# Attention with joined products for v's two parts, and one of eight pairs of heads weighed in float32

## What is computed

```python
q, k, v = (qkv[:, :, 0], qkv[:, :, 1], qkv[:, :, 2])          # 16 heads of 32
attn = jnp.einsum('bnhd,bmhd->bhnm', q, k) * SCALE
attn = jnp.where(causal, attn, NEG)
attn = jax.nn.softmax(attn, axis=-1)
out = jnp.einsum('bhnm,bmhd->bnhd', attn, v).reshape(B, N, C)
return _bitlinear(out, w_proj)      # rounds out to 8 bits by its row's maximum, w_proj to three values
```

## Time and profile before

| | us |
|---|---|
| median of 3 runs | 1661.09 (1660.46 to 1661.43) |
| the profiled execution | 1663.5 |
| its span on the core | 1661.7 |
| attention, first to last start of `row_max` | 67 to 508 |
| first matmul of the mixing stage | 556.9 |

### The profile page before, as it was taken

How to read it: one execution, slowest core, us unless ns; L and a number is a source line. 1 busy time by engine, 2 the same in 40 slices (tenths; PEclk the granted TensorE clock), 3 DMA queues, 4 the chain that set the end, 5 groups by cost and what they waited for, 6 DMA issues and landing times.

```text
span 1661.7 us, 27064 instructions
## 1 busy us (share of the span) xinstructions
PE 1519.7 (91%) x10503; PEld 876.0 (53%) x10581; DVE 1298.7 (78%) x1865; ACT 665.6 (40%) x1190; POOL 972.9 (59%) x706
## 2 busy tenths in 40 slices
PE   2698898989988678799999999999999999999998
PEld 2477777777776233344444444444444444444443
DVE  5698898899885579888778878887878878878621
ACT  4577777777767110322322222223222222232131
POOL 2378778887775356655645644654564465465242
PEclk9799999999999889999999999999999999999999
DMA  3544543645431611200120030020020020010000
GB/s 130 150 126 124 137 131 101 155 120 130 124 87 53 177 45 51 69 20 7 27 68 7 13 83 7 14 76 13 14 64 25 7 70 26 1 45 1 0 26 26
DMA packets 62048, 105.98 MB, mean 64 GB/s; under 512 B 7880, under 2 KB 14176, under 8 KB 61920
## 3 DMA queue, kind: packets, MB, share of 16 engines
q1 hardware_dynamic: 61728, 104.10, 23.3%
q10 hardware_dynamic: 192, 0.14, 0.1%
HBM read 50.74 MB, written 19.92 MB: 43 GB/s over the span
## 4 chain that ended last, share of the span: by engine, by line
PE 59%; DVE 4%; POOL 2%; issue 1%; ACT 0%; POOLq 0%; DVEq 0%
PE gu L665 20%; PE y L630 10%; PE gu L679 9%; PE y L633 3%; PE y L638 3%; PE gu L618 3%; PE y L637 3%; PE y L634 3%; PE y L636 3%; PE misc L645 1%; PE misc L655 1%; PE misc L594 1%; PE misc L538 1%; DVE z L975 1%; DVE oT L986 1%
## 5 line engine op out<-in xcount | busy, mean ns | idle before, releaser
L1440 POOL TENSOR_TENSOR pL<-pT,pH 128x768 f16<-128x768 f32 x128 | 220.1, 1721 | 90.1 <-PE pv L513 40.3
L1532 POOL TENSOR_TENSOR fuL<-fu,fuH 128x512 f16<-128x512 f32 x96 | 125.1, 1304 | 248.1 <-ACT fuH L1345 248.1
L630 PE MATMUL y<-kv,toep 128*128 128x512 f32 x496 | 242.6, 612 | 20.1 <-DVE z L975 17.9
L986 DVE TENSOR_REDUCE oT<-z 128x64 f32<-128x512 f32 x256 | 175.6, 686 | 8.8
L665 PE MATMUL gu<-fT,wg 128*128 128x512 f16 x768 | 181.4, 379 | 0.4 <-ACT fT L1364 0.4
L665 PE MATMUL gu<-fT,wu 128*128 128x512 f16 x768 | 181.4, 379 | 0.0
L982 DVE TENSOR_TENSOR z<-z,cT 128x512 f32<-128x512 f32 x112 | 168.2, 1502 | 3.8
L1345 ACT ACTIVATE fuH<-fu 128x512 f16<-128x512 f32 x96 | 60.2, 627 | 254.7 <-DVE fu L1001 254.7
L1191 ACT ACTIVATE pT<-s_kq,ws 128x768 f32<-128x768 f32 x128 | 115.3, 901 | 104.8 <-PE s_kq L493 104.8
L979 DVE TENSOR_TENSOR z<-y,shared 128x512 f32<-128x512 f32 x112 | 76.8, 686 | 90.8 <-PE y L634 76.9
L630 PEld LDWEIGHTS y<-kv,toep 128*128 128x128 f32 x496 | 92.7, 195 | 101.5 <-issue 62.0
(11 more groups left out here) (189 smaller groups left out, 3777.8 us busy)
## 6 DMA issues: line engine op xcount, KB each, us to landing
pack<-qkhl SPq DMA_DIRECT2D x256, 128.0 KB, 2.6
x_sb<-in_x SPq DMA_DIRECT2D x16, 512.0 KB, 4.7
c_sb<-in_ctx SPq DMA_DIRECT2D x32, 256.0 KB, 4.8
hankel<-in_L_xattn_k SPq DMA_DIRECT2D x32, 256.0 KB, 4.8
x_grp<-x_scratch SPq DMA_DIRECT2D x32, 256.0 KB, 4.0
out_y<-yo SPq DMA_DIRECT2D x32, 256.0 KB, 2.9
x_scratch<-x_sb SPq DMA_DIRECT2D x15, 512.0 KB, 3.0
wraw<-in_L_attn_w_qkv SPq DMA_DIRECT2D x3, 1024.0 KB, 9.9
```

Source lines behind the costliest of these rows:

```text
L630: made = T.matmul(to, tap(h, lb - kb), keys_values(h, kb, half), start=kb == 0, stop=kb == lb)
L986: V.tensor_reduce(out=oT[h % 2][:, lb, own].rearrange("p (b j) -> p b j", b=HB), in_=z[n % 2][:], op=ALU.add, axis=AXIS.X).then_inc(m_z, 1)
L1440: G.tensor_tensor(pL[n % 2][:], pT[n % NP][:], pH[n % NP][:], ALU.subtract).then_inc(low_done, 1)
L1532: G.tensor_tensor(fuL[:, ib, :], fu[n % 2][:], fuH[:, ib, :], ALU.subtract).then_inc(f_fl, 1)
```

## The change

It joins v's high and low part in one tile `vHL` of 65 columns (32 high, a one, 32 low), so that a block of probabilities takes two matmuls of 65 columns (`pH` and `pL` times both parts) where it took four. The two halves of the sum land apart in PSUM and in `oraw`, ACT copies 260 columns where it copied 132, and a new POOL instruction, `sum_parts`, adds them, once a batch, at step 8b+21. DVE's division moves from step 8b+21 to 8b+22, and waits for that sum (`o_sum`).

The pair p = 0 of each batch is weighed without a split: six float32 matmuls of 33 columns, straight from `pT` and a float32 v (`vW`). It has no high and no low part. The high part of p = 4 moves from DVE to ACT, so DVE has none left. `split_v` on DVE has three instructions where it had two (448, 64 and 448 columns where it had twice 512). `pT` has four buffers where it had three; the buffers of `fw_raw` go from three to two, so that SP's load of piece n waits for POOL to be through with piece n-2.

```diff
-    NX, NPACK, NP = 8, 3, 3
-    HIGH_ON_ACT = (1, 2, 3, 5, 6, 7)
+    NX, NPACK, NP, NPT = 8, 3, 3, 4
+    W_HEADS = 2
...
-        oraw = [q(f"oraw{i}", [P, NT, HEADS, VW], F32) for i in range(2)]
-        fw_raw = [q(f"fw_raw{i}", [P, PIECE], F32) for i in range(3)]
+        oraw = [q(f"oraw{i}", [P, NT, HEADS, VW + D], F32) for i in range(2)]
+        fw_raw = [q(f"fw_raw{i}", [P, PIECE], F32) for i in range(2)]
...
-        vH = [q(f"vH{i}", [P, NT, HEADS, VW], F16) for i in range(3)]
-        vL = [q(f"vL{i}", [P, NT, HEADS, D], F16) for i in range(3)]
+        vHL = [q(f"vHL{i}", [P, NT, HEADS - W_HEADS, VW + D], F16) for i in range(3)]
+        vW = [q(f"vW{i}", [P, NT, W_HEADS, VW], F32) for i in range(3)]
...
-        pT = [q(f"pT{i}", [P, 6, P], F32) for i in range(3)]
+        pT = [q(f"pT{i}", [P, 6, P], F32) for i in range(NPT)]
...
+        def whole(n):
+            return n % PAIRS == 0
...
             def weigh(n):
...
+                if whole(n):
+                    w.wait_ge(exp_done, n + 1)
+                    w.wait_ge(v_whole, 2 * b + 2)
+                else:
+                    w.wait_ge(high_done, n_split(n))
+                    w.wait_ge(low_done, n_split(n))
...
-                            T.matmul(acc[:, t, hh, :], ph[:, block, :], vh[:, mt, h, :], start=mt == 0, stop=False)
-                            T.matmul(acc[:, t, hh, 0:D], ph[:, block, :], vl[:, mt, h, :], start=False, stop=False)
-                            T.matmul(acc[:, t, hh, 0:D], pl[:, block, :], vl[:, mt, h, :], start=False, stop=False)
-                            made = T.matmul(acc[:, t, hh, :], pl[:, block, :], vh[:, mt, h, :], start=False, stop=mt == t)
+                            if whole(n):
+                                made = T.matmul(acc[:, t, hh, 0:VW], pT[n % NPT][:, block, :], vW[b % 3][:, mt, h, :],
+                                                start=mt == 0, stop=mt == t)
+                                continue
+                            v = vHL[b % 3][:, mt, h - W_HEADS, :]
+                            T.matmul(acc[:, t, hh, :], ph[:, block, :], v, start=mt == 0, stop=False)
+                            made = T.matmul(acc[:, t, hh, :], pl[:, block, :], v, start=False, stop=mt == t)
...
             def split_v(b, t):
...
+                V.tensor_scalar(vhl[:, :, 0:D], v[:, W_HEADS:, :], scale, None, ALU.mult).then_inc(v_high, 1)
+                V.tensor_scalar(vw[:, :, 0:D], v[:, 0:W_HEADS, :], scale, None, ALU.mult).then_inc(v_whole, 1)
...
-            def high_part(n):
-                w.wait_ge(exp_done, n + 1)
-                if n >= NP:
-                    w.wait_ge(pv_pe, n - NP + 1)
-                V.tensor_copy(pH[n % NP][:], pT[n % NP][:]).then_inc(high_dve, 1)
...
                 if k == 0:
                     w.wait_ge(pv_out, PAIRS * (b + 1))
                     chain.step(V.reciprocal(rl, oraw[b % 2][:, :, :, D]))
+                elif k == 1:
                     chain.wait()
+                    w.wait_ge(o_sum, b + 1)
...
             def exponentials(n):
...
-                if n >= NP:
-                    w.wait_ge(low_done, n - NP + 1)
+                if n >= NPT and whole(n - NPT):
+                    w.wait_ge(pv_pe, n - NPT + 1)
+                elif n >= NPT:
+                    w.wait_ge(low_done, n_split(n - NPT))
...
             def weighed(n):
...
+                width = VW if whole(n) else VW + D
+                h = heads_of(n)[0]
+                S.activation(oraw[b % 2][:, :, h:h + 2, 0:width], acc[:, :, :, 0:width], ACT.Copy).then_inc(pv_out, 1)
...
-                if (n := pair(t, HIGH)) is not None and n % PAIRS in HIGH_ON_ACT:
+                if (n := pair(t, HIGH)) is not None and not whole(n):
                     high_part(n)
...
+            def sum_parts(b):
+                raw = oraw[b % 2][:, :, W_HEADS:, :]
+                w.wait_ge(pv_out, PAIRS * (b + 1))
+                G.tensor_tensor(raw[:, :, :, 0:D], raw[:, :, :, 0:D], raw[:, :, :, VW:VW + D], ALU.add).then_inc(o_sum, 1)
...
             for t in STEPS:
-                if (n := pair(t, LOW)) is not None:
+                if (n := pair(t, LOW)) is not None and not whole(n):
                     low_part(n)
+                for b, k in batches(t, FINISH, 1):
+                    sum_parts(b)
...
                 wT_ready(w, 3)
-                if n >= 3:
-                    w.wait_ge(fw_taken, n - 2)
+                if n >= 2:
+                    w.wait_ge(fw_taken, n - 1)
```

More of the change, by code:

```diff
@@ L113, in decoder_kernel @@
         skips = sb(ctx, "skips", [P, M_HEADS, M_POS], F32)
-        rows_s = sb(ctx, "rows_s", [2 * IB, P], F32)
         GROUP = 4
@@ L247, in decoder_kernel @@
         st_pe, exp_done = signal("st_pe"), signal("exp")
-        high_act, high_dve, low_done = signal("p_high_act"), signal("p_high_dve"), signal("p_low")
+        high_done, low_done = signal("p_high"), signal("p_low")
+        v_whole, o_sum = signal("v_whole"), signal("o_sum")
         pv_pe, pv_out = signal("pv_pe"), signal("pv_out")
@@ L315, in decoder_kernel, with heads_of, n_split @@
         W_REST = range(min(len(weight_steps), W_STEPS), W_STEPS)
-        def high_done(n):
-            b, p = divmod(n, PAIRS)
-            if p in HIGH_ON_ACT:
-                return high_act, b * len(HIGH_ON_ACT) + HIGH_ON_ACT.index(p) + 1
-            other = [i for i in range(PAIRS) if i not in HIGH_ON_ACT]
-            return high_dve, b * len(other) + other.index(p) + 1
+        def whole(n):
+            return n % PAIRS == 0
+        def heads_of(n):
+            return 2 * (n % PAIRS), 2 * (n % PAIRS) + 1
+        def n_split(n):
+            return n - n // PAIRS
         def wT_ready(w, i):
@@ L484, in probabilities @@
                 w.wait_ge(mT_low, use + 1)
-                for hh in range(2):
-                    h = 2 * p + hh
+                for hh, h in enumerate(heads_of(n)):
                     for tile in range(2):
                         scores(s_kq[:, 2 * hh + tile, :], h, tile, tile, False)
-                    T.matmul(s_kq[:, 2 * hh:2 * hh + 2, :], pick[:, h % H_HEADS, :], nt[:, 0:N], start=False, stop=hh == 1)
-                for hh in range(2):
-                    h = 2 * p + hh
+                    T.matmul(s_kq[:, 2 * hh:2 * hh + 2, :], pick[:, 2 * (p % HP) + hh, :], nt[:, 0:N], start=False, stop=hh == 1)
+                for hh, h in enumerate(heads_of(n)):
                     scores(s_kq[:, 4 + hh, :], h, 0, 1, hh == 0)
-                    made = T.matmul(s_kq[:, 4 + hh, :], pick[:, h % H_HEADS, :], nt[:, P:N], start=False, stop=hh == 1)
+                    made = T.matmul(s_kq[:, 4 + hh, :], pick[:, 2 * (p % HP) + hh, :], nt[:, P:N], start=False, stop=hh == 1)
                 made.then_inc(st_pe, 1)
@@ L849, in weight_pieces @@
                 if not second and n < PIECES:
-                    raw, pw = fw_raw[n % 3], fw_pow[n % 2]
+                    raw, pw = fw_raw[n % 2], fw_pow[n % 2]
                     wT_ready(w, 3)
-                    w.wait_ge(fw_in[n % 3], 16 * (n // 3 + 1))
+                    w.wait_ge(fw_in[n % 2], 16 * (n // 2 + 1))
                     if n >= 2:
@@ L900, in vector_program @@
                         low_max(use)
-                if (n := pair(t, HIGH)) is not None and n % PAIRS not in HIGH_ON_ACT:
-                    high_part(n)
                 for b, k in batches(t, FINISH, 13):
@@ L1196, in high_part @@
                     w.wait_ge(pv_pe, n - NP + 1)
-                S.activation(pH[n % NP][:], pT[n % NP][:], ACT.Copy).then_inc(high_act, 1)
+                S.activation(pH[n % NP][:], pT[n % NPT][:], ACT.Copy).then_inc(high_done, 1)
             def weighed(n):
                 b, p = divmod(n, PAIRS)
-                acc = pv[:, 0:NT * 2 * VW].rearrange("p (t h w) -> p t h w", t=NT, h=2)
+                acc = pv[:, 0:NT * 2 * (VW + D)].rearrange("p (t h w) -> p t h w", t=NT, h=2)
                 w.wait_ge(pv_pe, n + 1)
@@ L1204, in weighed @@
                     w.wait_ge(o_mult, b - 1)
-                S.activation(oraw[b % 2][:, :, 2 * p:2 * p + 2, :], acc, ACT.Copy).then_inc(pv_out, 1)
+                width = VW if whole(n) else VW + D
+                h = heads_of(n)[0]
+                S.activation(oraw[b % 2][:, :, h:h + 2, 0:width], acc[:, :, :, 0:width], ACT.Copy).then_inc(pv_out, 1)
             def finish(b, k):
@@ L1624, in load_piece @@
                 wT_ready(w, 3)
[L1625 to L1627 removed]
+                if n >= 2:
+                    w.wait_ge(fw_taken, n - 1)
+                Y.dma_start(fw_raw[n % 2][:], (w_gate, w_up)[m][cb * P:(cb + 1) * P, o * PIECE:(o + 1) * PIECE]).then_inc(fw_in[n % 2], 16)
             def weight_pieces(k):
```

48 lines of the change are left out of this document (23 added, 25 removed).

## The result

The changed kernel takes 1664.7 us in the median of 14 runs (1660.8 to 1667.9), the kernel before 1661.1 (1659.6 to 1663.1): a ratio of 1.0019, interval 1.0011 to 1.0028. It is 3.7 us slower, where 10 us less were forecast. With 14 runs each, executions of one kernel spread by 0.2 to 0.4%, more than the 0.1% that three runs had suggested. The profiled span is 1663.2 against 1661.7, so the two traces show 1.5 of the 3.7.

A forecast was written before the change was run, and what follows sets the result against it. Attention was taken as bound by PE in about 76% of steps, by DVE in 24%. Savings of 0.86 us a batch, 13.8 over 16, less 1.2 (end) and 2.6 (clock), gave 10 off 1661: 1651 us, range 1640 to 1667.

The forecast's parts named there:

- the bunching of division and maximum: DVE, kind 6: both instructions (1.23 + 1.22 us), 0.95 for take_max and the scaling were said to fit in one step.
- The wait for DVE's maximum: PE's wait in attention for DVE's maximum, 31.1 us before, was to stay near 31 us or fall slightly.
- the third rival: Both savings, PE's and DVE's, count in full: 16 x 1.1 = 18 us less, 1641 us; chance 0.13.
- PE: Weighing: joined pairs 0.35 us each (0.25 saved), float32 pair 1.36 (0.77 more); 1.0 us less a batch.
- the upper bound of 0.192: Float32 pair on PE: if its weight loads don't overlap, 12 x 0.192 = 2.3 us, 1.7 more a batch.
- 0.76 less 0.3 for ACT: Per batch in attention: PE's 1.0 us counted in 76% of steps, minus 0.3 for waits on ACT's chain to xqT.
- DVE: 0.4 a batch: Of DVE's net saving of 1.25 us a batch, a third falls where DVE sets the step: 0.4.
- ACT: ACT gets 1.7 us more a batch; 0.3 charged, as PE's waits for xqT in kind 0 grow.
- The first rival: ACT becomes the bound, its 1.7 us a batch standing on the path: 1674 us, slower; chance 0.18.
- The new wait: DVE's division waits for sum_parts (1.9 us) on POOL; covered by 0.7 us, nothing counted except for the last batch.
- The end: Last batch's division, on the chain to the mixing stage, starts 1.2 us later; attention's last row_max near 496 instead of 508.
- The clock: PE's growing idle time lowers its granted clock in two such stretches more, at 1.3 us: 2.6 us lost.

The follow-up runs named there:

- no_sum_kind5: Changed kernel without sum_parts and its wait (products with v's low part missing from output), division back in kind 5 (step 8b+21): 1643.7 us, ratio 0.9896.
- no_sum_kind6: Changed kernel without sum_parts and its wait (products with v's low part missing from output), division left in kind 6 (step 8b+22): 1662.1 us, ratio 1.0003.

## Why the prediction was wrong

**The step that failed** is the sentence on DVE that priced the bunching of division and maximum at nothing: "which fits, since DVE is through early with kind 5". The numbers were against it: 0.95 + 1.23 + 1.22 and 0.68 for the scaling make 4.1 us, and PE needs 3.7 in a step of kind 6 and 2.9 in one of kind 7 (runs without pieces). By itself that excess of 0.4 costs nothing in the steady stretch; with a piece in the step or the one before it has no room left, and a DVE instruction that starts while POOL's is running waits it out (last section). That DVE is idle in kind 5 is of no use to kind 6, because `take_max` can't start before its scores are there, and the queue is in order. The move cost 18.4 us where the sum is left out; with the sum, 14.5 together with the sum's place. The wait for DVE's maximum, said to stay near 31 us, went to 35.6, and to 38.4 with that for `qkt`.

**The rest of the sum** stood nearer, and added up to about the third rival. Without the bunching and the sum the changed kernel is at 1643.7, 17.4 us under before (rival 3: 1641); I had 13.8 for it.

- PE: 0.36 a joined pair (forecast 0.35) and 1.26 for the float32 pair (1.36): right. By the rule on weight loads from the Trainium skill, "TensorE: Matmul & The Clock Gate", section "LDWEIGHTS (loading the stationary operand)", columns / 1.2 ns, the records would be 0.107 apart; the trace agrees, with 0.105. As to the bounds, the upper bound of 0.192 was wrong. What reached the steps is 0.35 a batch without pieces, against 0.76 less 0.3 for ACT, 0.46. Into kinds 7, 0 and 1 nothing was saved.
- DVE: 0.4 a batch was too small. With pieces `no_sum_kind5` gains 14.3 us in the steady stretch (350.2 to 335.9), 1.2 a batch, of which PE has 0.35. The rest, over 0.8, is twice what I gave DVE. Part of it is the clock, whose cost between 100 and 488 us falls from 8.3 to 3.4 us; which part isn't separated.
- ACT: the wait for `xqT` stayed at 2.5 us with pieces and went from 3.6 to 5.8 without. Together with those for `oraw` and `pT` it grew by 5.8 us without pieces, 0.4 a batch: right in size. The first rival, ACT as the bound, had the right sign and the wrong engine.
- The new wait: in the steady stretch nothing waited for `o_sum`, as forecast. Behind it the last three divisions waited 0.14, 4.65 and 1.51 us, where I had allowed for the last alone. The sum took 1.79 us (forecast 1.9). I had counted nothing for it in the steps; its 2.6 us are hardly clear of noise, and the traces of the changed kernel and `no_sum_kind6` have 1.8 of them in the steady stretch.
- The end, against the earlier trace rows:

```profile
535.32 0.35 DVE L831 RECIPROCAL osmall<-oraw 128x32 f32<-128x32 f32 x1 [5.82 <-ACT oraw L1215]
535.36 1.73 POOL L1455 TENSOR_TENSOR oraw<-oraw 128x896 f32<-128x896 f32 x1 [1.47 <-ACT oraw L1215]
537.18 1.23 DVE L837 TENSOR_TENSOR o_sb<-oraw,osmall 128x1024 f32<-128x1024 f32 x1 [1.51 <-POOL oraw L1455]
...
543.74 3.42 PE L541 MATMUL misc<-wprojT,oqT 128*128 128x512 bf16 x8 [0.83 <-ACT oqT L1240]
```

The division starts 1.86 us after the reciprocal where it was 0.70: 1.2 later, as forecast. What was missed is the clock behind it: the projection takes 3.42 us at a granted clock of 0.55 where it took 1.89 at 1.00. Attention was 1.4 us ahead at the last `row_max` (506.96 against 508.38, not 496), and the mixing stage starts at 558.33, 1.4 late. So the bunching ate up the gain, and the loss that the two traces show lies wholly behind the last `row_max`: 51.4 us from there to the mixing stage where it was 48.5.

- The clock: two stretches more were allowed for, 2.6 us. Between 100 and 488 us it took up to 8.3 before and 10.0 after, and the projection's 1.5 come to it: about right.

## What to carry to other kernels

Where engines run in lockstep, one step at a time, a move is priced by the fullest step it makes, not by the engine's mean load or by idle time in the step before: add up every instruction of that queue between two of the instructions the other engine waits for, the optional ones too, and compare with the other engine's step. A long optional piece of work in such a queue should be cut up and spread before anything is shaved off the main work; here that gave 16 to 23 us, more than the change could. And when several small results may be summed later, start the sum early for all but the last, so that what depends on it needn't move.

## What the runs showed of the hardware

DVE waits for POOL's running instruction, inside its own duration. The second instruction of a weight piece, first in the kernel before with POOL idle, then in the changed kernel beside the sum:

```profile
332.25 0.43 DVE L857 TENSOR_SCALAR fw_pow<-fw_pow 128x512 f32<-128x512 f32 x1
...
329.86 1.93 POOL L1455 TENSOR_TENSOR oraw<-oraw 128x896 f32<-128x896 f32 x1
330.23 1.85 DVE L865 TENSOR_SCALAR fw_pow<-fw_pow 128x512 f32<-128x512 f32 x1
```

The same instruction takes 0.43 or 1.85 us, and in the second case ends 0.3 after POOL's. That is no accident: of its 24 instances in the changed kernel 17 take 1.37 to 1.85 us, and all of these end 0.28 to 0.29 after a POOL instruction that was running when they started; the other seven take 0.43, with no POOL instruction of more than two columns beside them. The longest five divisions (1.73 to 2.60 us) end 1.08 to 1.09 after such a one. It holds the other way too: a `low_part` begun 0.19 us into the division at 130.64 takes 2.62 us in place of 1.64, and ends 1.50 after it. So these instructions are not slowed evenly: their time is what it is alone, plus the wait for the other's end. Taking the sum away (`no_sum_kind6`) brings the group's mean from 1474 to 1223 ns, but that of L863 goes from 937 to 1043 and that of the division from 1363 to 1491: what meets what is shuffled, and the three together fall by only 1.4 us in the stretch from 110 to 484. A mean duration of such an instruction is therefore a mean over two cases, and what it costs depends on which POOL instruction is running when it starts. The division had 1.23, 1.75 and 2.60 us in the lines above. The maximum of `o_sb`, with one input, stays at 1.21 to 1.22 in all of them. The Trainium skill, "GPSIMD Engine Reference", section "1. Specifications", says that the SBUF interfaces are shared and that DVE instructions with two SBUF inputs, or in a mode that uses two ports, contend for them; the division, with two, and the maximum agree with it, and the page gives no price.

The clock fell behind waits. After PE's waits of 1.06 and 1.91 us for step 46 the 3.4 us from 222.0 had 0.59, nearly the 1.2 GHz level. Spreading the pieces cut the longest wait from 2.6 to 1.5 us in the kernel before, and it fell in no stretch from 100 to 488 us any more. This is worth up to 8 us, beside 12 of waits. That nothing but the waits brings the clock down is not tested.
